# The second image's first norm power moved from ahead of the 15th to ahead of the 13th indirect store in GpSimd's stream

## The reference

```
x = conv_attention(x)                    # group norm, 4 heads over 1024 points, softmax, projection, + x
t = tokens(x)                            # (2, 1024, 128)
t = t + linear_attention(layernorm(t))   # softmax of the keys over the tokens and of the queries over 16 dims,
                                         # context = K V^T, att = context^T Q, projection
t = t + moe(layernorm(t))                # router softmax over 8 experts, top 2 of them;
                                         # per expert: layernorm * g + b, W1 (128x512), gelu, W2 (512x128)
```

## Time and profile before

| | us |
|---|---|
| median of 3 runs | 363.89 (363.23 to 364.35) |
| span of the profiled execution, from its first to its last instruction | 384.2 |
| PE busy in it | 334.2 |
| POOL busy in it | 110.8 |

### The profile page before, as it was taken

How to read it: one execution, slowest core, us unless ns; L and a number is a source line. 1 busy time by engine, 2 the same in 40 slices (tenths; PEclk the granted TensorE clock), 3 DMA queues, 4 the chain that set the end, 5 groups by cost and what they waited for, 6 DMA issues and landing times.

```text
span 384.2 us, 6582 instructions
## 1 busy us (share of the span) xinstructions
PE 334.2 (87%) x2004; PEld 211.5 (55%) x2004; DVE 202.1 (53%) x616; ACT 204.4 (53%) x324; POOL 110.8 (29%) x140
## 2 busy tenths in 40 slices
PE   7879799899999989999998496967551999999996
PEld 3533343333333335445432354867551999999996
DVE  2584444563756553565576248666402455777620
ACT  1460765666576554655585023665212677777732
POOL 2082291000000001000307630061774344444430
PEclk9985989999999999999999879996665899999999
DMA  6078768660000025000001102010211222222415
GB/s 186 2 149 194 170 146 333 154 243 34 0 2 3 3 72 149 0 2 1 2 0 43 55 8 62 16 28 23 62 62 34 64 72 70 71 66 79 143 37 210
DMA packets 21772, 29.28 MB, mean 76 GB/s; under 512 B 4055, under 2 KB 15628, under 8 KB 21484
## 3 DMA queue, kind: packets, MB, share of 16 engines
q1 hardware_dynamic: 16808, 18.04, 17.7%
q0 software_dynamic: 3744, 10.31, 8.4%
q10 hardware_dynamic: 1188, 0.53, 0.6%
HBM read 11.62 MB, written 9.25 MB: 54 GB/s over the span
## 4 chain that ended last, share of the span: by engine, by line
PE 70%; DVE 13%; issue 6%; another core or an unknown queue 4%; ACT 3%; DMA 1%; POOL 1%; DVEq 0%; SPq 0%; ACTq 0%; POOLq 0%
PE ps L864 15%; PE ps L1081 10%; PE ps L1068 9%; PE ps L845 6%; PE ps L826 6%; DVE above L1189 4%; PE ps L706 2%; PE ps L806 2%; PE ps L922 2%; PE ps L746 2%; PE ps L899 2%; PE ps L778 1%; PE ps L891 1%; DMA Qs<-mrow 1%
## 5 line engine op out<-in xcount | busy, mean ns | idle before, releaser
L558 ACT ACTIVATE probs<-ps 128x1024 f32<-128x1024 f32 x64 | 65.3, 1021 | 37.0 <-PE ps L845 36.9
L1081 PE MATMUL ps<-w,GT 128*128 x368 | 55.0, 297 | 18.8 <-ACT GT L684 15.0
L864 PE MATMUL ps<-probs,vT 128*32 128x512 f32 x256 | 68.2, 608 | 1.1 <-ACT probs L558 1.1
L864 PE MATMUL ps<-probs,ones 128*32 128x512 f32 x256 | 68.2, 609 | 0.0
L1081 PEld LDWEIGHTS ps<-w,GT 128*128 128x128 f32 x368 | 49.3, 208 | 22.0 <-issue 21.7
L1189 DVE CUSTOM_DVE_ANT_0 above<-ps,above 128x512 f32<-128x512 f32 x56 | 38.7, 691 | 40.8 <-PE ps L826 39.0
L496 POOL DMA_INDIRECT token_out<-Y,yidx x46 | 44.2, 961 | 48.2 <-DVE Y L1480 46.6
L433 POOL TENSOR_TENSOR rstd<-ve,minus_half 128x1 f32<-128x1 f32 (+2 forms) x6 | 10.3, 1724 | 160.6 <-DVE ve L1231 88.6
L1068 PE MATMUL ps<-XTT,w1s 128*128 128x128 f32 x368 | 53.1, 291 | 3.2 <-issue 3.2
L684 ACT ACTIVATE GT<-H 128x512 f32<-128x512 f32 x46 | 28.9, 629 | 46.5 <-DVE H L1469 27.4
L1068 PEld LDWEIGHTS ps<-XTT,w1s 128*128 128x128 f32 x368 | 49.2, 208 | 4.3 <-issue 4.3
(11 more groups left out here) (196 smaller groups left out, 427.5 us busy)
## 6 DMA issues: line engine op xcount, KB each, us to landing
expert_in<-zeros POOLq DMA_DIRECT2D x2, 1495.0 KB, 7.6
XR<-expert_in SPq DMA_DIRECT2D x46, 65.0 KB
Qs<-q_hi SPq DMA_DIRECT2D x16, 128.0 KB, 3.1
w<-in_L_ffn_W SPq DMA_DIRECT2D x1, 2048.0 KB, 8.4
w<-in_L_ffn_W SPq DMA_DIRECT2D x8, 256.0 KB, 4.1
YG<-token_out SPq DMA_DIRECT2D x8, 256.0 KB, 4.1
Ks<-k_hi SPq DMA_DIRECT2D x14, 128.0 KB, 2.6
X<-in_x SPq DMA_DIRECT2D x2, 512.0 KB, 4.6
```

Of the source, the lines that this page charges most:

```text
L558: nc.scalar.activation(probs[:, s % 3, :], bank(2 + 2 * (s % 2), 2), ACT.Exp).then_inc(exp_done, 1)
L864: last = nc.tensor.matmul(bank(6 + o % 2)[i * HD:(i + 1) * HD, :], w, probs[:, s % 3, hd * HALF:(hd + 1) * HALF], start=kt == 0, stop=kt = ...
L1081: last = nc.tensor.matmul(bank(4 + p)[:, 0:D], GT[:, p, c, :], w2[:, e, c, :], start=c == 0, stop=c == HC - 1)
```

## The change

One number in one line: the call of `between` that holds `rsqrt(B + 2)` is made for group 6 in place of group 7.

```
-            scatter(0, lambda j: rsqrt(B + 2) if j == J - 1 else None)
+            scatter(0, lambda j: rsqrt(B + 2) if j == J - 2 else None)
             rsqrt(B + 3)
```

## The result

The changed kernel takes 360.82 us (median of 6 runs, 360.41 to 361.41), the kernel before 363.34 (361.95 to 364.35, 6 runs). The ratio is 0.9932, with a 95% interval of 0.9913 to 0.9951: 0.7% faster, 2.5 us. The direction was forecast.

A forecast was written before the change was run, and what follows sets the result against it. It took the chain from the second image's power through its second layer, then 40 tiles of PE work, as the bound. Power 2.2 us sooner, later tiles costing 0.7, sum -1.5: 363.9 to 362.4 us, range 361.4 to 364.7.

The forecast's parts named there:

- the timed runs don't have the waits for nothing: Four late starts on ACT and DVE during indirect stores, up to 11.12 us, were taken as missing in timed runs.
- the 20.3 us: Whole kernel: the first profile's span of 384.2 against the median of 363.89, at least 20.3 us not in timed runs.
- a gap between two ways of counting: Whole kernel: a rival reading, profile total against reported time, about 6.2 us, leaving 14.1 us to waits; no chance given.
- The place of the power: POOL, second image: the power waits for store 14 though the variance is ready; moved up, it starts 2.2 us sooner.
- The cost of the later tiles: Tile loads behind two more stores come 2.53 us later against the power; `keys_exp` on ACT loses 0.7 us.
- the cover on ACT: ACT's idle times of 1.08 and 0.39 us ahead of the two exponentials, said to hide 1.8 us of later tiles.
- the bound on the gain: Second image's queries on PE: less idle time could add up to 1.7 us, at most -3.5 in all, counted unlikely.
- The clock's part: PE at the second image's queries: less idle time, higher clock, up to 1.7 us further gain; 361 us, chance 0.06.
- The profile's order holds: Rival at POOL's power: it waits for DVE in both kernels, only later tiles count; +0.7, 364.6 us, chance 0.13.
- Half the gain: Rival: late exponential or slow projection stays in timed runs; power gains 1.2 to 0.4, about 363.7 us, chance 0.17.
- Slower: Rival at PE's tiles: no gain at the power, longer wait for tile 0 lowers the clock; 365.9 us, chance 0.12.

The follow-up runs named there:

- the new profile of before: The kernel before, unchanged, run and profiled once more: 363.65 us (10 runs), ratio 1.0015; the profiled execution took 364.49 us.
- the other profile: The changed kernel, unchanged, run and profiled again beside other versions: 360.90 us (6 runs), ratio 0.9907 to the kernel before.

## Why the prediction was right and where it was wrong

**Reading the first profile.** The step "the timed runs don't have the waits for nothing" was right, and it decided the sign. Both the new profile of before and all later ones are free of them, with spans of 357 to 363. In the 12 profiles that have both, the span is 1.7 to 1.9 us *shorter* than the time of the same execution, so the 20.3 us were not a gap between two ways of counting either. What made those waits in one execution isn't known; no experiment was aimed at it.

**The place of the power.** Forecast: 14th store ends 2.2 us behind the variance, gain 2.2. Measured: 11.47 - 9.62 = 1.85 us. The mechanism is right. The size was 0.35 too large, since the power follows a store without the 0.2 us that I put there (218.75 + 0.96 = 219.71, power at 219.73), and since the variance was 0.2 later than worked out (ACT's copy of the second half took 0.60 us and not 0.54, and DVE's statistics ended 0.90 us behind it and not 0.82: 215.96 + 0.60 = 216.56, 215.69 + 1.77 = 217.46).

**The cost of the later tiles.** Forecast: 0.7. Measured: 12.27 - 11.95 = 0.3 (0.2 with the 12.15 of the other profile). ACT starts the keys' exponentials 0.95 us behind the queries', not 1.06. And the second transpose is done 10.92 us behind the power (229.03 + 0.33 - 218.44), not 11.22: the tiles' landing had 0.3 us of slack where I had read none. That the cover on ACT was nearly used up was right: the next two stores cost 2.7 us (2.5 with the clock held).

**The step that failed** is the bound on the gain: "A further gain has no row of its own: PE would sit idle for some 2 us less ahead of the second image's queries ... at most -2.53 + 0.7 - 1.7 = -3.5. That end I count as unlikely." The clock's part had a chance of 0.06, and the sum and the range left it out. In the profiles it is there: 13.64 - 11.95 = 1.69 us, with L922 at 5.41 and 3.72, won in the kernel before by two fillers and lost in the changed kernel by taking three away. The rows for it stood in the prediction: a projection that took 3.78 us behind 5.12 us of idle time against 2.05, a clock of 0.53 behind 2.79 us, and a pause of some 2 us, which the prediction itself names. I priced the clock as a risk on the side of a loss and didn't put the same row on the side of the kernel *before*, which is where the pause was.

What the clock's part is worth in timed runs stays open. Two more fillers in the kernel before gained 0.5 us, by the interval at most 1.0. Three fewer in the changed kernel lost 1.5. And with all pauses filled, the place of the power alone was worth 2.2 us by the medians, more than the 1.5 (1.85 - 0.32) that the profiles give it. Place and clock are both shown; how the 2.5 us divide between them is not.

Sum at the keys' exponentials: -1.85 - 1.69 + 0.32 = -3.2 us. The medians differ by 2.5 us. In the profiles the ends differ by more, not less (362.7 - 208.26 = 154.4 and 359.7 - 208.82 = 150.9 us behind the start of ACT's last exponential), but these two executions took 364.49 and 361.41 us, each the longest of its set, and the clock's low stretches later on fall differently in each profile (granted 0.94 in 245 to 300 before, 0.88 in the changed kernel). So a difference between two profiles can't be laid beside one between medians to a few tenths, and I leave the remaining 0.7 open.

**The rivals.** "The profile's order holds" is out: POOL's power starts right behind the 14th store in every profile with 14 stores ahead of it but the first. "Half the gain" is out too: in the new profile of before ACT's last exponentials come at their usual 0.64 us of idle time, the projection takes 2.05 us, and the variance is done at 217.78, 1.93 us ahead of the 14th store's end. "Slower" is out for this change; its mechanism, later tiles, is what makes the power ahead of the 11th store useless. Nothing held up the two stores that now stand behind the power as well: the last two took 0.95 and 0.96 us, as those ahead of it did.

## What to carry to other kernels

Lay the span of a profile beside the timed runs before reading a single wait in it; if they differ by more than the rest of the runs scatter, look for waits that no engine ends, and work out the timed run without them. Where an engine issues a row of transfers and one short instruction that others wait for, the short one belongs at the first place where its input is there, and no further up: each transfer ahead of it costs one issue (1.26 us here), each behind it delays whoever waits for the last one. When a change closes a pause of PE, price the clock of the matmuls behind the pause in both kernels, and take the price from timed runs: one profile each showed 1.7 us where the medians moved by 0.5 and, in the other kernel, by 1.5.

## What the runs showed of the hardware

- One execution had waits of DVE and ACT of up to 11.12 us that end on nothing in the profile, behind matmuls of PE that by their rows were long over (DVE started 4.27 us behind one), while indirect stores were under way. Its span was 384.2 in place of 362.7. Not one of the 12 other profiles has this.
- PE's granted clock for 16 matmuls behind a pause: full behind pauses of 0.39 to 0.91 us (3.72 us), lower behind 2.19 and 2.97 us (5.41 us in both). The length of that one pause doesn't decide: eight transposes behind 2.79 us took 1.97 us in the kernel before and 1.09 with two more fillers ahead, and behind some 1.2 us they took 1.88 in the changed kernel (1.23) and 1.09 with four fillers behind the keys (1.19, power ahead of the 11th store). Adding 0.9 us of matmuls that nobody reads to each of two pauses of 1.6 and 1.2 us made the kernel 1.5 us faster, in two batches.
- An indirect store of 128 rows takes 1.26 us from start to start on POOL, and a short instruction behind one starts 0.02 us after its end.
